# The sparse branch's part of W_o: from a TensorE product per head to a VectorE row addition per head and one product at the end

## What is computed

```python
# attention block, x: 1024 x 256, 16 heads
attn = softmax(causal(q k^T * scale)) v            # per head, 128 columns of v
sparse_out = so @ W_io                             # a small branch on 8 selected tokens for each of 8 index heads
io = sparse_out.mean(axis=2)[:, :, None, :VD]      # 8 index heads x 128 numbers, the same for all 1024 tokens
io = jnp.repeat(io, NH // IH, axis=1)              # each serves two of the 16 heads
attn = attn + io
out = attn.transpose(0, 2, 1, 3).reshape(B, S, NH * VD) @ W_o
# then layernorm(x + out), an MLP with ternary weights, layernorm
```

## Time and profile before

| | before |
|---|---|
| median of 3 runs | 727.49 us (726.06 to 728.73) |
| the profiled execution | 727.64 us |
| its span in the trace | 725.9 us |
| PE busy | 665.2 us (92%) |
| VectorE busy | 469.2 us (65%) |
| ACT busy | 397.7 us (55%) |
| POOL busy | 365.8 us (50%) |
| all `tc` transposes on PE (L701) | 88.0 us, 576 of 280 ns |
| all `PTl` differences on VectorE (L1058) | 102.5 us, 192 of 554 ns |
| VectorE's wait for ACT's `PTh` | 75.1 us |

### The profile page before, as it was taken

How to read it: one execution, slowest core, us unless ns; L and a number is a source line. 1 busy time by engine, 2 the same in 40 slices (tenths; PEclk the granted TensorE clock), 3 DMA queues, 4 the chain that set the end, 5 groups by cost and what they waited for, 6 DMA issues and landing times.

```text
span 725.9 us, 14196 instructions
## 1 busy us (share of the span) xinstructions
PE 665.2 (92%) x4496; PEld 604.1 (83%) x4496; DVE 469.2 (65%) x1293; ACT 397.7 (55%) x940; POOL 365.8 (50%) x313
## 2 busy tenths in 40 slices
PE   5666799999999999999999999999999999898895
PEld 5646689888988898889888888898889888887895
DVE  2675256666766576666666666666656677895895
ACT  3342254756475647565656565656565658544562
POOL 5522254835474447445744575356536644530563
PEclk9866599999999999999999999999999999999998
DMA  6142310371036103710361037103610373000000
GB/s 203 46 130 75 79 51 1 88 154 52 1 89 153 51 0 87 152 51 0 87 152 51 0 87 152 51 0 87 151 51 0 87 217 87 2 1 1 1 31 30
DMA packets 28719, 50.51 MB, mean 70 GB/s; under 512 B 8976, under 2 KB 19472, under 8 KB 28688
## 3 DMA queue, kind: packets, MB, share of 16 engines
q1 hardware_dynamic: 28688, 50.12, 27.5%
HBM read 15.50 MB, written 1.05 MB: 23 GB/s over the span
## 4 chain that ended last, share of the span: by engine, by line
PE 60%; DVE 13%; ACT 12%; issue 10%; POOL 4%; DMA 1%; DVEq 0%; ACTq 0%; POOLq 0%; SPq 0%
PE J L675 10%; PE J L677 9%; PE J L676 9%; PE J L701 4%; DVE PTl L1058 4%; ACT kvraw L1022 3%; PE SC L692 3%; PE SC L690 3%; PE SC L689 3%; PE SC L691 3%; PE SC L688 3%; POOL rstd L607 3%; ACT Pb L959 3%; ACT PTh L941 2%; PE SC L866 2%
## 5 line engine op out<-in xcount | busy, mean ns | idle before, releaser
L1058 DVE TENSOR_TENSOR PTl<-J,PTh 128x512 fp32r<-128x512 f32 (+1 forms) x192 | 102.5, 554 | 75.1 <-ACT PTh L941 74.4
L959 ACT ACTIVATE Pb<-SC,nm 128x128 f32<-128x128 f32 (+7 forms) x128 | 94.8, 740 | 47.0 <-DVE nm L1121 46.2
L1121 DVE CUSTOM_DVE_ANT_0 SC<-SC,mask 128x128 f32<-128x128 f32 (+7 forms) x128 | 97.4, 761 | 28.7 <-PE SC L692 27.1
L941 ACT ACTIVATE PTh<-J 128x512 fp32r<-128x512 f32 (+1 forms) x192 | 88.3, 492 | 10.3 <-PE J L701 9.5
L701 PE MATMUL J<-ident,Pb 128*128 128x128 f32 x576 | 88.0, 280 | 4.7 <-ACT Pb L959 4.5
L675 PE MATMUL J<-PTh,Vh 128*128 128x256 f32 x320 | 88.0, 275 | 4.0 <-DVE PTl L1058 3.8
L676 PE MATMUL J<-PTl,Vh 128*128 128x256 f32 x320 | 89.6, 280 | 0.0
L677 PE MATMUL J<-PTh,Vl 128*128 128x256 f32 x320 | 89.3, 279 | 0.0
L701 PEld LDWEIGHTS J<-ident,Pb 128*128 128x128 f32 x576 | 64.8, 142 | 11.2 <-ACT Pb L959 5.4
L688 PE MATMUL SC<-KNh,QNh 128*128 128x512 f32 (+1 forms) x192 | 69.1, 360 | 0.0
L675 PEld LDWEIGHTS J<-PTh,Vh 128*128 128x128 f32 x320 | 60.2, 188 | 9.0 <-DVE PTl L1058 6.7
(11 more groups left out here) (267 smaller groups left out, 1916.7 us busy)
## 6 DMA issues: line engine op xcount, KB each, us to landing
KD<-RKh SPq DMA_DIRECT2D x32, 256.0 KB, 4.5
KL<-RKl SPq DMA_DIRECT2D x32, 256.0 KB, 5.1
KX<-KX SPq DMA_DIRECT2D x16, 256.0 KB, 2.4
QX<-QX SPq DMA_DIRECT2D x16, 256.0 KB, 2.4
QS<-RQh SPq DMA_DIRECT2D x16, 256.0 KB, 4.0
QS<-RQl SPq DMA_DIRECT2D x16, 256.0 KB, 4.5
r_kv<-in_L_attn_W_ckv SPq DMA_DIRECT2D x8, 384.0 KB, 3.4
r_qn<-in_L_attn_W_qT SPq DMA_DIRECT2D x16, 128.0 KB, 2.7
```

The source lines that it names most:

```text
L941: return act.activation(o, i, ACT.Copy)
L959: act.activation(Pb[i % 2][:, w], SC[i % 2][:, w], ACT.Exp, bias=nm[:, i % 2:i % 2 + 1], scale=-1.0, accum_out=sm[:, b, i:i + 1]).then_inc ...
L1058: dve.tensor_tensor(o, i, h.bitcast(F32), ALU.subtract).then_inc(done[kind], 1)
L1121: dve.tensor_tensor_reduce(out=SC[i % 2][:, w], in0=SC[i % 2][:, w], in1=mask[:, 128 * (7 - i):S], scale=-SCALE, scalar=HIGH, op0=ALU.add, ...
```

## The change

`rw` takes no product and no bank any more. VectorE multiplies the 128 x 256 block `r_o` (W_o as loaded, not split) row by row with the 128 numbers in `iocol` and adds it to `row` (`scalar_tensor_tensor`). So `row` now holds 128 different rows, whose sum over partitions is what is wanted. A new step `rwt`, one per launch, in the second half of `LAST` ahead of `rowadd`, multiplies `row` with a 128 x 128 block of ones on PE in plain fp32 and copies the result back to `row`. The high and low parts of the sparse output go away. SP's load of the next W_o waits until VectorE has read the last one (`rw_done`); POOL's split waits for `ab` in place of `rw`; and the second head's load moves behind the stacks in SP's part of the prologue.

```diff
-                  "rw", "wtot", "ht", "h2")}
+                  "rwt", "wtot", "ht", "h2")}
@@
-               "vs": 1, "pv": 4, "wo": 4, "side": 11, "tc": NCH, "wb": 1, "rw": 1, "wtot": 3, "ht": 2}
+               "vs": 1, "pv": 4, "wo": 4, "side": 11, "tc": NCH, "wb": 1, "rwt": 1, "wtot": 3, "ht": 2}
@@
-                    add(0, True, ("wtot", 0, 2), ("rowadd", 0, 0), ("rowadd", 0, 1))
+                    add(0, True, ("wtot", 0, 2), ("rwt", 0, 0), ("rowadd", 0, 0), ("rowadd", 0, 1))
@@ SP
                     wait(sp, wo_split, u)
+                    wait(sp, rw_done, u)
                     sp.dma_start(r_o[:, :], W_o[bass.ds(u * NOPE, NOPE), :]).then_inc(ld_o, 16)
...
             load("wqn", 1)
-            load("wosp", 1)
...
             stack("stq", 0, 0, 0)
+            load("wosp", 1)
@@ POOL
-                        split(ld_o, 16 * u + 16, r_o[:, :], Woh[:, :], Wol[:, :], wo_hi, wo_split, ready["rw"], u, u)
+                        split(ld_o, 16 * u + 16, r_o[:, :], Woh[:, :], Wol[:, :], wo_hi, wo_split, ready["ab"], u, u)
@@ PE
-                if kind == "rw":
-                    pe.wait_ge(io_ready, p + off // 2 + 1)
-                    pe.wait_ge(wo_split, u + 1)
-                    last = three(o[:, 0:D], iocol[:, 0:1].to_broadcast([128, 128]), iocol[:, 1:2].to_broadcast([128, 128]), Woh[:, :], Wol[:, :], True, True)
+                if kind == "rwt":
+                    pe.wait_ge(rw_done, NH)
+                    last = mm(o[:, 0:D], lhsT=onesf[:, :], rhs=row[:, :], start=True, stop=True)
@@ VectorE
-                            dve.tensor_copy(ioThl[:, :, 0], ioT[:, :]).then_inc(io_hi, 1)
-                            dve.wait_ge(io_hi, 1)
-                            dve.tensor_tensor(ioThl[:, :, 1], ioT[:, :], ioThl[:, :, 0].bitcast(F32), ALU.subtract).then_inc(io_hi, 1)
-                            dve.wait_ge(io_hi, 2)
-                        pair = ioThl[:, bass.ds(u, 1), :].rearrange("p a n -> p (a n)")
-                        dve.tensor_copy(iocol[:, :], pair.bitcast(F32)).then_inc(io_ready, 1)
+                        dve.tensor_copy(iocol[:, :], ioT[:, bass.ds(u, 1)]).then_inc(io_ready, 1)
                     if kind == "rw":
...
-                        dve.wait_ge(ready["rw"], u + 1)
-                        dve.tensor_tensor(row[:, :], o[:, 0:D], row[:, :], ALU.add).then_inc(done["rw"], 1)
+                        dve.wait_ge(io_ready, p + off // 2 + 1)
+                        dve.wait_ge(ld_o, 16 * u + 16)
+                        hold(dve, rw_done, u)
+                        dve.scalar_tensor_tensor(row[:, :], r_o[:, :], iocol[:, 0:1], row[:, :], ALU.mult, ALU.add).then_inc(rw_done, 1)
+                    if kind == "rwt":
+                        dve.wait_ge(ready["rwt"], 1)
+                        dve.tensor_copy(row[:, :], o[:, 0:D]).then_inc(done["rwt"], 1)
                     if kind == "rowadd":
-                        dve.wait_ge(done["rw"], NH)
+                        dve.wait_ge(done["rwt"], 1)
```

More of the change, by code:

```diff
@@ L113, in attention_and_mlp @@
         ioT = sb("ioT", [128, IH])
-        ioThl = sb("ioThl", [128, IH, 2], F32R)
-        iocol = sb("iocol", [128, 2], F32R)
+        iocol = sb("iocol", [128, 1])
         row = sb("row", [128, D])
@@ L231, in attention_and_mlp @@
                 ("xt", "qc", "qm", "kv", "kpe", "qp", "kt", "ab", "qn", "vs", "pv", "wo", "side", "tc",
-                 "wb", "rw", "wtot", "ht", "h2")}
+                 "wb", "rwt", "wtot", "ht", "h2")}
         ld_mlp = [sem(f"ld_mlp{n}") for n in range(3)]
@@ L260, in attention_and_mlp @@
         tp_ready, pt_lo = ready["tc"], done["tc"]
-        io_hi, io_ready = sem("io_hi"), sem("io_ready")
+        io_ready, rw_done = sem("io_ready"), sem("rw_done")
         row_added = sem("row_added")
@@ L278, in unit @@
         def unit(kind, off, p):
-            if kind in ("wtot", "ht"):
+            if kind in ("wtot", "ht", "rwt"):
                 return off
@@ L960, in run @@
                                        scale=-1.0, accum_out=sm[:, b, i:i + 1]).then_inc(exp_done, 1)
-                    if kind in ready and kind not in ("side", "wb", "wtot", "wo", "rw", "h2"):
+                    if kind in ready and kind not in ("side", "wb", "wtot", "wo", "rwt", "h2"):
                         act.wait_ge(ready[kind], count(kind, u, c))
```

## The result

The changed kernel takes 731.05 us (median of 18 executions, 727.87 to 735.63), the kernel before, beside it, 727.21 (724.59 to 729.14): a ratio of 1.0056, 95% interval 1.0039 to 1.0073, so +3.8 to +4.1 us. Its profiled execution took 728.15 with a span of 726.4, the low end of its own runs.

What follows compares the result with a forecast made beforehand. PE was taken to bound the kernel, busy 665.2 of 725.9 us, with waits behind ACT and VectorE evictions. Terms -2.45 + 5.1 - 0.95 + 0.8 + 0.3 = +2.8 on 727.49 gave 730.3; range 725.5 to 733.5.

Steps and rivals of the forecast that it cites:

- One sign: Sign of being right: P times V of the head's last tile starts about 1.2 us behind PE's score tile end.
- one sign of being wrong: Would show the forecast wrong: PE waiting for a weight split, which no PE wait of the earlier trace was on.
- part 4: Prologue: PE can start the second pair's k product at 90.8 against 91.75; gain 0.95 us, bounds 0 and 1.7.
- Parts 1 and 5, first halves: First-half products leaving PE save 0.35 us each: -2.45 in seven pairs; last pair +0.3, as a collision may cost 1.
- Part 2: Second half: PE's earlier arrival is lost as VectorE's row addition precedes the last score tile's minimum, only 0.12 us earlier.
- Part 3: Pair boundaries: chunk 10 takes chunk 8's PSUM bank and waits for its lo difference; +0.73 us each, seven make +5.1.
- Part 5, the end: Last pair: plain fp32 `rwt` product makes P times V about 0.4 us later, its VectorE copy takes 0.4; +0.8 taken.
- The clock: No term in the sum; the earlier trace's one clock fall may come or go, 1.8 us either way.
- the boundary is covered: PE reaches chunk 10 no earlier than chunk 8's eviction ends, so only removed products count: -5.7, 721.7 us; chance 0.12.
- A wash: The pair boundary costs only the 0.35 us that one product saves: 727.6 us; chance 0.2.
- The clock falls at the boundary: PE idle about 1.5 us or more there lowers the clock: 733.8 us if in two of seven, 742.7 in all; chance 0.1.
- Port collision: POOL's rope starts before the row addition; PE loses 0.2 to 0.5 in each of eight pairs: 732 to 734; chance 0.1.

Runs made afterwards that it cites:

- the repeated kernel before: The kernel before, unchanged, run again for its granted clocks and spans: 724.94 us, 0.9999 of before.
- the wait alone: Kernel before, all products kept, PE also waiting ahead of chunks 10 and 11 for the lo difference two chunks back: 732.83 us, 1.0101 of before.
- the fillers apart: Changed kernel with each pair's two filler steps put where the removed steps stood, none at the pair's end: 724.17 us, 0.9966 of before.
- two buffers: Changed kernel with a second buffer for loaded W_o rows and the second head's load early again, fillers still at the pair's end: 730.35 us, 1.0039 of before.
- the late addition: The fillers apart, with the second half's row addition moved on VectorE behind the last score tile's minimum: 723.25 us, 0.9946 of before.

## Why the prediction was right, and where it was not

Forecast 730.3 with a range to 733.5, measured 731.05. The direction, the mechanism and the place were right: in the trace of after the transposes of chunk 10 wait for a lo difference at each of seven boundaries, and the distance of the row additions grew by 0.46, within the 0.2 to 0.6 that the text named. The first score tile starts at 80.29, in a trace whose prologue runs 2.6 us ahead of that of the earlier trace rows (79.87 against 82.44 at the product before it): 82.9, the "near 83" of the text. One sign doesn't fit: P times V of the head's last tile starts 4.2 us behind the end of PE's score tile (519.27, 523.50), not 1.2, and the text's own working (520.46, 524.12) didn't give 1.2 either. And one sign of being wrong did appear, a wait of PE for a weight split, once, in the prologue; part 4 has it.

The terms, measured from the two traces that agree in their first 80 us (the repeated kernel before, span 722.4, and the changed one, 726.4). The same product in the repeated kernel before and in the changed one, in the first pair and in the last:

```profile
97.69 0.39 PE L675 MATMUL J<-qch,ABh 128*128 128x512 f32 x1
...
609.01 0.40 PE L675 MATMUL J<-qch,ABh 128*128 128x512 f32 x1
```

```profile
97.13 0.40 PE L675 MATMUL J<-qch,ABh 128*128 128x512 f32 x1
...
613.01 0.39 PE L675 MATMUL J<-qch,ABh 128*128 128x512 f32 x1
```

- Parts 1 and 5, first halves: 0.29 to 0.40 in each of eight pairs (0.35 at the product itself), -2.7 where -2.45 and +0.3 were put. Right for seven. In the last pair the collision with POOL that was given 1 us didn't come.
- Part 2, the second half's gain is lost to VectorE: right, and shown in the traces from both sides. PE came 0.66 early, the minimum followed the addition at 0.40, as computed from the `acc` rows. Counted from the pair's first half product, which is 0.73 early, it starts 0.03 earlier than before (516.69 and 0.73 make 517.42, against 517.45), where 0.12 was put.
- Part 3, the boundary: +0.78 on average for the seven (0.64 to 0.84), where 0.73 stood. (The text's 0.53 between ACT's copies should be 0.49 by the earlier trace rows, 2.06 less 0.60 over three; the sum doesn't hang on it.) From 97.69 to 609.01 the changed kernel lost 4.56 against the repeated one: 7 times 0.45 and one fall of the clock of 1.4; with the first halves' 0.34 added back, 0.78. Sum +5.5 against +5.1.
- Part 4, the prologue: -0.95 forecast, -0.1 measured. This step failed. The text put 3.4 us from issue to landing, the median of eight loads, and let SP issue the load ahead of the stacks; it landed in 4.3, and POOL started 0.26 behind that. The text had even named what is queued behind it, and not asked what that does to the load in front; the one load of the eight at this place had taken 5.3.
- Part 5, the end: +0.8 forecast, 0.0 measured. The first 0.4 was right where it was put: P times V behind the product starts 0.44 later. What the text left out is the next P times V, which had waited 0.79 for VectorE and now waits 0.39, so nothing is left of it. The copy on VectorE (0.41) and `rowadd`, 0.4 more in the text, were hidden.
- The clock: +1.4 in this trace (no digit of the page's clock line shows it), forecast zero, with the remark that one fall of 1.8 may come or go. The repeated kernel before has no such fall; the execution of the earlier trace rows, from which the forecast started, has one too, at 660 us. The window of the changed kernel (busy of PE in us, granted clock, DMA share, GB/s) stands at half, the lower level of 1.2 GHz:

```profile
608.20:611.60 3.40, 3.31 (x11) 0.52 0.87 289
```

Measured sum: -2.7 + 5.5 - 0.1 + 0.0 + 1.4 = +4.1, against 4.0 between these two executions. Without the fall it is +2.7, and the forecast's was +2.8: what was put too low (the prologue by 0.85, the boundary by 0.4) and what was put too high (the end by 0.8, the first halves by 0.55) cancel out. The forecast was right in its main term and lucky in the small ones. The medians show 1.1 to 1.4 us more than 2.7. The table has 3.0 for the executions at 0.962 or above, so most of it goes with the clock, of which the forecast had nothing; that the change itself brings more falls isn't shown.

The rivals: *the boundary is covered* is refuted by the wait alone and by the fillers apart. *A wash* is refuted: 0.45 a pair remains. *The clock falls at the boundary* is true as a possibility, not as a rule. It fell at one of seven in one trace and at none in the changed kernel's; a fall 14 us behind the last boundary, in three traces of four, remains open. In the changed kernel windows of 8 us around all seven boundaries, each with 1.8 us of idle, show 1.00. The Trainium skill, TensorE: Matmul & The Clock Gate, "HAM oscillation", has every wait between bursts put the clock back; it tells of a kernel whose waits were longer, some 3 to 5 us for a DMA, and here the waits of 1.6 us left the clock up at all seven. *Port collision* didn't happen, because its condition didn't: POOL was at work ahead of none of the sixteen additions, and all took 473 to 485 ns:

```profile
L1256 DVE SCALAR_TENSOR_TENSOR row<-r_o,iocol,row x16: 473/476/485, 81.0 to 614.7; 128x256 f32<-128x256 f32 x16
```

In seven of them POOL's rope started 0.19 us after the addition had:

```profile
541.42 0.48 DVE L1256 SCALAR_TENSOR_TENSOR row<-r_o,iocol,row 128x256 f32<-128x256 f32 x1
...
541.61 2.55 POOL L556 TENSOR_TENSOR KX<-KX,CS 128x1024 f32<-128x1024 f32 x1 [8.57 <-DMA KX<-KX]
```

By the rule of the Trainium skill, SBUF — State Buffer, "Who interferes with whom", POOL would be held for the addition's remaining 0.29. The rope took 2.55 where it took 2.40: 0.15 more, so some of it, and nobody waits for it. The other order came up at `rowadd`, whose pieces also have both sources in SBUF: three of them started while POOL's L637 was at work. One (635.24, 0.27 behind POOL's start, 1.3 before its end) took 0.96; the other two took 0.68, as without POOL. So VectorE was held up by 0.28 once and never for the rest of a POOL operation.

Open: why two buffers alone gave 12 low clocks of 12 and the late addition 10 of 12 (the kernel before, in that batch, 12 of 27), when both together with the fillers apart gave 2 of 9. What was seen is that the clock fell behind a wait of 1.67 us (two buffers, one boundary) and one of 2.7 (fillers apart, prologue; its window is below), that waits of 1.6 us elsewhere left it at 1.00, and that the kernel with the addition late had the prologue's wait at 2.6 and kept 1.00 behind it. What decides between them no run here tells apart. First the window of the fillers apart, then the wait of the addition late:

```profile
92.00:96.00 4.00, 4.00 (x20) 0.50 0.06 15
```

```profile
PE J L677 <- POOL Wckl L603: 2.6, 1, 2.6
```

## What to carry to other kernels

Where buffers are dealt out in turn, count what an edit does to the deal before counting what it saves: two steps less and two fillers at another place made a step wait for an eviction two steps back, and cost twice what the removed products gave in the trace (5.5 against 2.7 us). A filler belongs where the removed step stood. Work that moves to another engine goes behind that engine's next critical operation, not ahead of it: 0.40 us a pair in the traces here. And a single buffer that is now also read by VectorE holds up the queue that refills it.

## What the runs showed of the hardware that was not expected

- The times of one program spread by some 9 us (723.07 to 732.34), and the median goes with the mean granted clock: 725.6 us at 0.962 or above and 728.1 below, for the unchanged kernel, in 85 executions. Part of the spread isn't in that mean: the start of the kernel, where products stood 0.21 us apart until 9.8 us in one execution and until 18.4 in another, counts as 1.00.
- A fall of 3.4 us at the lower level cost 1.4 us in the changed kernel (608 us) and 1.0 with two buffers (the pair around 375 us took 74.70 us where its neighbours took 73.65 to 73.80). One of about 6.8 us, in the prologue with the fillers apart, cost 3.1: from the k product to the pair's first half product 10.89 us (90.38, 101.27), and 7.75 (89.92, 97.67) in the kernel with the addition late. On the page's line of tenths the one at 608 us doesn't show.
- Plain fp32 with 256 columns went as two instructions, and P times V behind it started 0.44 us later at the upper level of the clock (2.4 GHz): the 0.44 that had been scaled from rows at a mostly lower one.
- A DMA of 384 KB landed in 3.3 to 3.4 us in five of the six pairs of the kernel before, where SP issued nothing for 3.5 us or more behind it (in the sixth, where the next issue came 2.8 behind, it took 6.9, for no reason that the trace shows). In the changed kernel, with loads of 256 KB issued 0.6 us behind it on the same queue, it took 4.2 to 4.9 in the pairs and 4.3 in the prologue.
